# One layer stack on one core: the branch on the mask flag taken earlier, and the queries of the second cross attention split in two steps by two engines

## The reference

```python
x = x + _L0_xattn_ref(_layernorm(x), ctx, ctx, mask_bk0, ...)      # 16 heads of 16, tanh capped
x = x + _L0_attn_ref(_layernorm(x), w_qkv, b_qkv, ..., w_proj, b_proj)
x = x + _L0_ffn_ref(_layernorm(x), weight)
x = x + _L1_xattn_ref(_layernorm(x), ctx, ctx, mask_bf1, Wq, bq, ...)
x = x + _L1_attn_ref(_layernorm(x), ...)
x = x + _L1_ffn_ref(_layernorm(x), ...)
...
# _L0_ffn_ref: ternary weights, activations rounded to 8 bits
a_scale = max(abs(x), axis=-1) + EPS
y = round(clip(x / a_scale * 127, -128, 127)) @ w_quant.T * (w_scale * a_scale / 127)
# _L1_xattn_ref, per head
scores = where(mask, q @ k.T / sqrt(16), -1e9)
out = softmax(scores) @ v
```

## Time and profile before

| | us |
|---|---|
| median of three runs | 748.99 |
| lowest and highest | 747.96, 749.51 |
| the profiled execution | 750.28 |
| its span (first to last instruction) | 748.6 |

### The profile page before, as it was taken

How to read it: one execution, slowest core, us unless ns; L and a number is a source line. 1 busy time by engine, 2 the same in 40 slices (tenths; PEclk the granted TensorE clock), 3 DMA queues, 4 the chain that set the end, 5 groups by cost and what they waited for, 6 DMA issues and landing times. The chain is left out here.

```text
span 748.6 us, 14468 instructions
## 1 busy us (share of the span) xinstructions
PE 646.4 (86%) x4972; PEld 390.7 (52%) x4972; DVE 413.4 (55%) x903; ACT 464.5 (62%) x558; POOL 71.9 (10%) x148
## 2 busy tenths in 40 slices
PE   1698777878788769898589999999999899988997
PEld 1354444444445345575235555555555567754886
DVE  6576352231322315865578898988883426446443
ACT  3899969999999974472036676767767046303100
POOL 3010201000100003000110101111110200000000
PEclk9999979999999999999758999999999999999899
DMA  5787765384433114000802332323230740000000
GB/s 132 217 245 212 232 205 168 105 239 152 143 112 109 49 25 151 1 1 0 287 9 72 86 81 76 88 79 84 77 83 2 241 139 1 2 0 1 0 1 14
DMA packets 52694, 73.39 MB, mean 98 GB/s; under 512 B 10866, under 2 KB 29618, under 8 KB 52658
## 3 DMA queue, kind: packets, MB, share of 16 engines
q1 hardware_dynamic: 51890, 72.19, 33.0%
q10 hardware_dynamic: 768, 0.73, 0.3%
HBM read 58.89 MB, written 12.85 MB: 96 GB/s over the span
## 5 line engine op out<-in xcount | busy, mean ns | idle before, releaser
L1575 DVE TENSOR_REDUCE sb_m_blk<-ps 128x1 f32<-128x512 f32 x256 | 159.6, 683 | 22.8 <-PE ps L1432 21.7
L1383 ACT ACTIVATE sb_probs<-ps 128x1024 f32<-128x1024 f32 x128 | 125.9, 1025 | 52.9 <-PE ps L1462 51.7
L651 ACT ACTIVATE sb_probs<-ps 128x1024 f32<-128x1024 f32 x128 | 124.0, 1016 | 16.5 <-PE ps L697 14.2
L655 ACT ACTIVATE sb_probs<-sb_probs,sb_neg_cap,sb_cap 128x4096 f32<-128x4096 f32 x32 | 121.6, 3801 | 1.1
L714 PE MATMUL ps<-sb_probs,sb_v_st 128*32 128x256 f32 x1024 | 77.5, 400 | 41.1 <-ACT sb_probs L655 38.7
L1432 PE MATMUL ps<-sb_k_st,sb_q_m 96*128 96x512 bf16 x256 | 91.4, 402 | 2.7 <-DVE sb_m_blk L1575 2.0
L697 PE MATMUL ps<-sb_q_st,sb_k_st 112*128 112x256 bf16 x512 | 76.6, 285 | 5.9 <-DMA sb_k_st<-k_parts_l 4.2
L1462 PE MATMUL ps<-sb_q_st,sb_k_st 115*128 115x256 bf16 x512 | 77.7, 275 | 1.4 <-ACT sb_probs L1383 1.4
L697 PEld LDWEIGHTS ps<-sb_q_st,sb_k_st 112*128 112x128 bf16 x512 | 46.2, 101 | 49.7 <-ACT sb_probs L651 23.8
L1478 PE MATMUL ps<-sb_probs,sb_v_st 128*32 128x256 f32 x1024 | 67.7, 385 | 0.2 <-ACT sb_probs L1383 0.2
L714 PEld LDWEIGHTS ps<-sb_probs,sb_v_st 128*32 128x32 f32 x1024 | 24.2, 110 | 70.4 <-ACT sb_probs L655 49.3
(11 more groups left out here) (264 smaller groups left out, 875.0 us busy)
## 6 DMA issues: line engine op xcount, KB each, us to landing
sb_k_st<-k_parts_l SPq DMA_DIRECT2D x223, 64.0 KB, 2.0
sb_k_st<-k_parts_l SPq DMA_DIRECT2D x93, 128.0 KB, 3.2
k_parts_l<-sb_v_proj SPq DMA_DIRECT2D x24, 256.0 KB
k_parts_l<-sb_early SPq DMA_DIRECT2D x48, 128.0 KB
sb_v_proj<-ctxT_blocks SPq DMA_DIRECT2D x8, 512.0 KB, 8.9
sb_early<-ctxT SPq DMA_DIRECT2D x7, 512.0 KB, 4.0
sb_v_rows<-ctx_by_pair SPq DMA_DIRECT2D x7, 512.0 KB, 3.9
sb_k_st<-k_parts_l SPq DMA_DIRECT2D x64, 32.0 KB, 1.8
```

The costliest lines, as they stand in the source:

```text
L651: a.activation(probs[:, j % 2, 4 * g:4 * g + 4, :], scores_bank(g), ACT.Tanh).then_inc(s["tanh"], 1)
L655: a.activation(probs[:, j % 2], probs[:, j % 2], ACT.Exp, bias=k.neg_cap[:, 0:1], scale=k.cap[:, 0:1]).then_inc(s["exp"], 1)
L1383: sc.activation(probs[:, g], scores_bank(g), ACT.Exp).then_inc(s["exp"], 1)
L1575: v.tensor_reduce(k.m_blk[:, b, q, blk:blk + 1], k.ps[:, m_bank(m_turn_of(idx)), :], AX.X, ALU.max).then_inc(s["m_read"], 1)
```

## The change

Three things move.

- **The branch.** The block of the cross attention now begins right after the projection of the self attention. TensorE's `keep_busy` of eight and the one of four ahead of the branch go; behind the branch stands a `keep_busy` of four matmuls of half the columns (256). The norm, the rounding, the two transposes and the ternary linear move behind the barrier, on TensorE behind the branch. Five `keep_busy` matmuls stand ahead of the wait for `c_xn`, and two behind the query linear.
- **The split.** VectorE scales and splits heads 0 and 1 only (`x_two`, `split_rows1`, the copies in pairs), then scales the rest; GpSimd runs the same six operations for the other 14 heads. ScalarE's two copies go.
- **The turn.** TensorE turns heads 0 and 1 into bank 4 (`turn_first`, four transposes), and ScalarE copies both with all 115 rows straight to `q_st`, from which the first maxima are computed; GpSimd's two copies L1331 for heads 0 and 1 go. The other 14 heads are turned in two pieces, behind the maxima matmul 10 (12 transposes) and 13 (16), after a wait for GpSimd.

The core of the diff:

```diff
-            keep_busy(k, 8, 6)
-            pe.wait_ge(k.sem("c_aq"), 1)
...
+def split_rows1(vec, link, src, dst, done):
+    n = dst.shape[1]
...
+    twice = src.unsqueeze(2).to_broadcast([P, n, 2, DH])
+    link(vec.tensor_copy(pair(0), twice))
+    link(vec.tensor_tensor(src, src, one(0), ALU.subtract))
+    link(vec.tensor_copy(pair(1), twice))
+    link(vec.tensor_tensor(src, src, one(1), ALU.subtract))
+    link(vec.tensor_copy(dst[:, :, LOROW:STACK], one(0)))
+    vec.tensor_copy(pair(2), twice).then_inc(done, 1)
...
             stage(0, 0, True)
             stage(1, 1, True)
+            pool.wait_ge(s["rows"], 1 + QT)
+            split_rows1(g, link, q_rest, k.q_rows1[:, FIRST_ROWS:], s["copies"])
             m_parts(0, 0)
             m_parts(1, 1)
+            pool.wait_ge(s["q_stack"], H // 4)
...
             def all_heads(masked):
+                keep_busy(k, 4, 6, D)
+                pe.wait_ge(k.sem("c_aq"), 1)
...
+                rows_linear(k, k.a_qT, KT, k.w_tern, None, 3, k.sem("c_y"))
+                keep_busy(k, 5, 6)
                 pe.wait_ge(k.sem("c_xn"), QT)
                 transpose_rows(k, k.xn, 2, k.sem("c_xnT_ps"))
                 pe.wait_ge(k.sem("c_xnT"), 1)
                 rows_linear(k, k.xnT, KT, k.w1_q, None, 3, k.sem("d_q"))
-                pe.wait_ge(s["rows"], 4)
-                pe.wait_ge(s["copies"], 2)
-                turn(0)
+                keep_busy(k, 2, 6)
+                pe.wait_ge(s["rows"], 1)
+                turn_first()
                 for idx in range(n_m):
                     m_scores(0, 0, idx, masked, True, True)
-                    if idx in (1, 3, 5):
-                        turn((idx + 1) // 2)
+                    if idx in (10, 13):
+                        turn(2 * (idx // 3) - 6)
+                        turn(2 * (idx // 3) - 5)
...
-            keep_busy(k, 4, 6)
             masked = pe.value_load(k.masked_i[0:1, 0:1], min_val=0, max_val=1)
```

More of the change, by code:

```diff
@@ L924, in rows_linear, with keep_busy @@
     last.then_inc(done, 1)
-def keep_busy(k, n, bank):
+def keep_busy(k, n, bank, cols=2 * D):
     for _ in range(n):
-        k.nc.tensor.matmul(k.ps[:, bank, :], k.ones_sq[:, :], k.w1_o[:, :, :].rearrange("p t n -> p (t n)"), start=True, stop=True)
+        k.nc.tensor.matmul(k.ps[:, bank, 0:cols], k.ones_sq[:, :], k.w1_o[:, :, :].rearrange("p t n -> p (t n)")[:, 0:cols], start=True, stop=True)
 def update_pe(k, pe, tag, src, n_k, w, turn, norm=True):
@@ L1386, in body, with m_rows @@
                     if not (last and b == 1):
-                        m_rows(2 * it + b + 1, 1 - b)
-            def m_rows(h, b):
+                        m_rows(2 * it + b + 1, 1 - b, first and b == 0)
+            def m_rows(h, b, fresh=False):
                 act.wait_ge(s["m_turned"], h + 1)
-                act.wait_ge(s["q_staged"], h + 1)
+                if fresh:
+                    act.wait_ge(s["q_first"], 1)
+                else:
+                    act.wait_ge(s["q_staged"], h - 1)
                 sc.activation(k.q_st[MAXROW:LOROW, b, :], k.ps[MAXROW:LOROW, 0, 0:S], ACT.Copy).then_inc(s["m_rows"], 1)
@@ L1404, in _, with turn_first @@
             t = nc.tensor
+            def turn_first():
+                for h in range(2):
+                    for q in range(QT):
+                        last = t.transpose(turned(ACC_BANK)[:, (h * QT + q) * P:(h * QT + q + 1) * P],
+                                           k.q_rows1[:, q * 2 + h, :], k.ident_bf[:, :])
+                last.then_inc(s["q_turned"], 1)
             def turn(n):
+                pe.wait_ge(s["copies"], 1)
                 for h in range(4):
+                    if 4 * n + h < 2:
+                        continue
                     for q in range(QT):
                         last = t.transpose(turned(n)[:, (h * QT + q) * P:(h * QT + q + 1) * P],
-                                           k.q_rows1[:, q, 4 * n + h, :], k.ident_bf[:, :])
+                                           k.q_rows1[:, FIRST_ROWS + q * (H - 2) + 4 * n + h - 2, :], k.ident_bf[:, :])
                 last.then_inc(s["q_turned"], 1)
@@ L1431, in m_scores @@
                 key0 = (blk % (m_blocks // 2)) * 512
-                last = t.matmul(o, k.q_m[0:MAXROW, b, q * P:(q + 1) * P],
+                qs = k.q_st if first and h < 2 else k.q_m
+                last = t.matmul(o, qs[0:MAXROW, b, q * P:(q + 1) * P],
                                 k.k_st[0:MAXROW, 2 * b + blk // (m_blocks // 2), key0:key0 + 512], start=True, stop=not masked)
```

96 lines of the change are left out of this document (42 added, 54 removed).

## The result

| | us |
|---|---|
| changed kernel, median of five runs | 741.93 |
| lowest and highest | 740.33, 743.73 |
| before, median of five runs beside them | 748.99 (747.96 to 749.66) |
| ratio | 0.991, interval 0.989 to 0.993 |
| profiled execution of the changed kernel, its span | 741.93, 740.1 |

The changed kernel is 7.06 us faster; the forecast was 4.1. The granted clock over the span rose from 0.963 to 0.974 of full speed. The profiled executions differ by 8.35, since the one of before lay 1.29 above its median.

What follows compares the result with a forecast made beforehand. One chain between TensorE and VectorE, 349.53 to 388.68, was taken to bound the kernel. Gains 0.1 + 2.1 + 2.1 - 0.4, plus 0.2 for ScalarE's copy, make 4.1: 748.99 to 744.9 us, range 741.3 to 748.6.

Steps and rivals of the forecast that it cites:

- The branch: TensorE at the moved branch: load waits for queued matmuls, same 3.63 us, resumes at 353.5; gain 2.8 if clock holds.
- Rival 2: Load doesn't wait for matmuls; the whole 7.29 us from block entry are the branch; 748.0 us, chance 0.12.
- costed at nothing: GpSimd's zeroing and `v_st` copies under VectorE's norm, SyncE's 16 loads, and the branch's fetch meeting them: no cost booked.
- The clock over the gap: Clock falls over the new 4.0 us gap, half for 4.1 us of dense work; L293 at 365.6, gain 0.1.
- The query linear and what surrounds it: L293 to VectorE's scale, at full clock behind the five `keep_busy`: 3.4 us, before 5.55; gain 2.1.
- The split of two heads: Queries ready to first maxima matmul, heads 0 and 1 only: 3.5 us instead of 5.57; gain 2.1.
- GpSimd's split: Other 14 heads on GpSimd: 6.2 us, just hidden before TensorE needs it; at upper bound 9.1, 2.6 us show.
- The turns: Two later turns between head 0's maxima, half clock for the first and part of the second: 11.6 us, loss 0.4.
- The loop: Heads' loop behind head 0's maxima: nothing booked in the forecast sum; a changed period would show the prediction wrong.
- rival 4: The gain is given back in the loop (clock's phase, loads of head 2): 749.0 us, chance 0.08.
- the first: Rival: the clock holds over the new gap at the moved branch; gain 7.0, 741.9 us, chance 0.17.
- the third: Rival: GpSimd's split takes 12.4 us, twice its price; 6.0 wait ahead of the first turn, 750.9 us, chance 0.08.

Runs made afterwards that it cites:

- the delayed split: Changed kernel with a useless GpSimd zeroing of 2048 elements (1.87 us) ahead of its split; one execution, 748.92 us, sixteenth maximum at +40.90.
- the experiment above: Changed kernel with weights' loads late, four keep_busy ahead of the flag's load, GpSimd's value buffers after the rounded rows, three full keep_busy behind the branch: 739.30 us (0.987).
- the second profile: Changed kernel itself, unedited, timed and profiled again in the last session: median 743.33 us (0.991), profiled execution 745.08, sixteenth maximum at +39.63.

## Why the prediction was right, and where its steps were not

The time came out 3 us below the forecast and inside the range. The direction was right, the make-up of the sum was not.

- **The branch: the step failed.** I read the packets at 363.0, 1 us behind the end of the queue, as a load that waits until TensorE's matmuls are done, and took 3.63 us for the price. The price runs from the block's entry and the matmuls ran beside it: 7.29 us in before (358.43 to 365.72), 7.15 in after (349.86 to 357.01), 4.35 without the loads. The packets came late because of the loads, not because of the drain. Rival 2 had this mechanism and its numbers to a few tenths (resume at 357.15, transposes at 360.9). I had its chance at 0.12, on an argument that fitted both readings: I noted that the weights' loads were in the queues, under "costed at nothing", and didn't ask what the packet was waiting for. What decided it was how long the packet comes behind the entry in a place without loads: 1.9 us, with matmuls queued or without.
- **The clock over the gap: the fall was right, its length too long.** It fell at about 354 and was back about 361. The five `keep_busy` were to take 4.1 us of half clock, and saw none of it (4.46 in all, at full clock 4.6 by the estimate). The dense work began with the short `keep_busy` at 357.0, so the time that I allowed had passed by then. That is why rival 2's consequence was too dark: L293 came at 366.82 and not at 368, 1.1 late instead of 2.3.
- **The query linear and what surrounds it.** From L293 to VectorE's scale 3.55 (366.82 to 370.37), forecast 3.4, before 5.55. Right, gain 2.0.
- **The split of two heads.** From the scale to the first maxima matmul 3.12 (370.37 to 373.49), forecast 3.5, before 5.57. Gain 2.4 instead of 2.1; ScalarE's one copy at 372.84 was on time.
- **GpSimd's split.** 5.83, forecast 6.2: casts 0.95 (1.08), subtractions 1.03 and 1.02 (0.96), copy 0.57 (0.54). The row of the same shape was the right one to scale. It ended 8.55 behind the scale (forecast 9.1) and the turn began 8.93 behind it (9.4). That it was "just hidden" is confirmed by the delayed split, with 0.5 to spare.
- **The turns.** Head 0's maxima took 10.42 (373.92 to 384.34), forecast 11.6, before 11.2. The twelve transposes took 1.49, 0.8 forecast at full clock and 1.6 at half; the sixteen took 1.06, as at full clock. Half clock thus hit one turn, and VectorE stalled once, for 0.62. A loss of 0.4 was booked and a gain of 0.8 came.
- **What was costed at nothing.** GpSimd's zeroing and copies under VectorE's norm weren't free: the rounded rows came at 357.43 and not at 356.7, and the experiment above puts 0.66 on them. It cost the changed kernel nothing only because TensorE came 3.15 later still (360.58). SyncE's loads, in the same list, were the dear item: they are what the branch waited for.
- **The loop.** Nothing was booked for it as the forecast; rival 4 had it as a loss. It gave 2.70 in both profiled executions, by the clock in the first heads' scores. The rows that spoke for it were in the earlier trace rows: half clock in 386.5 to 396.7 costs as much wherever it goes away.

The sum to the sixteenth maximum is -1.1 + 2.0 + 2.4 + 0.8 = 4.1, and with 0.22 less from the first maxima matmul to the first maximum 4.37 measured, against 4.1 forecast: the agreement is luck, that of two errors, a branch that gave 1.2 less and turns and split that gave 1.5 more. In the second profile it is 3.24. The remaining 3 us of the median were booked nowhere in the forecast. The profiles show 2.7 in the loop, which goes with the clock there; how often each kernel has it, and how much of the rest is scatter of the other stages, isn't shown.

Some sums of the prediction don't come out as they stand, none of which moves the forecast: its slow end, 2.6 us above 744.9, is 747.5 and not 747.3; rival 2, with L293 2.3 late and the later gains of 4.0 that the sum has, would give 747.3 and not 748.0; and GpSimd's copies of `v_st` run 31.7 us earlier (383.69 to 351.97), only the zeroing about nine.

Of the rivals: the first (741.9 us) has the measured time and not the mechanism, since the clock did fall over the gap; the second has the mechanism of the branch and not the time; the third's mechanism lies half a microsecond away; the fourth went the other way.

## What to carry to other kernels

Put a branch to code that isn't loaded where the engine still has more than 4.4 us of queued work (four `keep_busy` of 3.67 hid all but 0.65), and issue no bulk loads at that moment: this alone, one line, gave the kernel before 4.5 us of the changed kernel's 7. When a gap "by issue" stands behind a branch, time it from where the engine's sequencer met the branch, not from where its last matmul ended. Split the work of the first consumer from the rest, and look up how much room the slower engine has: here it was 0.5 us, and a delay of 1.9 made VectorE's stall 1.6 longer. Take a second profile before a difference of 1 us between two profiles is read as an effect: two of the changed kernel differed by 1.13 in the chain and by 3.2 in the span.

## What the runs showed of the hardware

- An instruction fetch for a branch on TensorE: 1.9 us from the entry into the block to the packet without other DMA traffic (351.37 - 349.44), 4.7 to 4.8 with SyncE's 16 loads issued in the same moment (354.55 - 349.86, 363.26 - 358.43), and 2.4 to 2.5 from the packet to the first matmul in both.
- A register load and a branch proceed beside matmuls that are already queued; the flag's load alone showed 0.94 us.
- Two of VectorE's operations on two elements, both TENSOR_TENSOR, took 0.45 us instead of 0.16 while GpSimd copied in SBUF, and the TENSOR_SCALAR between them kept its 0.15: 0.66 us in all in a chain of 6.89. One operation took 1.00 instead of 0.22 beside a zeroing.
- The granted clock fell for 3.4 us in one kernel just behind the start of dense work (358.4 to 361.8), after 5.5 us in which TensorE was 55% busy; it stayed full in another whose TensorE list and loads there are the same and in which GpSimd starts later, so that TensorE waited 0.60 instead of 1.30 for the rounded rows. Each has one profile. And over the same code of the first heads it was full in some kernels' profiles and half in others', at 2.7 us. What sets this isn't settled.
